# Expert weights of a graph-MoE kernel: adjacent matrix rows per partition, and operands read with a column step

## The reference

```python
logits = x @ Wg + bg
vals, idx = jax.lax.top_k(logits, TOP_K)
gates = jax.nn.softmax(vals, axis=-1)
...
h1 = jax.nn.gelu(jnp.einsum('ecd,edh->ech', h, w1) + b1[:, None, :], approximate=False)
h2 = jnp.einsum('ech,ehd->ecd', h1, w2) + b2[:, None, :]
...
return jnp.zeros((N, D), x.dtype).at[tok_s].add(g_s[:, None] * y_s)
```

## Time and profile before

| | us |
|---|---|
| median of 3 runs | 3404.27 |
| lowest and highest run | 3402.09, 3410.98 |
| the profiled execution's own time | 3410.98 |
| its span, first to last instruction | 3410.9 |
| expert stage in it | 657 (2560 to 3217) |

### The profile page before, as it was taken

The page is one execution under the profiler, slowest core; times in us unless marked ns, Lnnn a source line. Parts: engine busy times, 40 slices in busy tenths (PEclk is TensorE's granted clock), DMA queues, the critical chain, the costliest instruction groups (busy, mean ns, idle before and its releaser), DMA issues.

```text
span 3410.9 us, 46164 instructions
## 1 busy us (share of the span) xinstructions
PE 2063.6 (61%) x10294; PEld 1676.9 (49%) x10295; DVE 1397.3 (41%) x3217; ACT 527.2 (15%) x1404; POOL 2391.6 (70%) x2216
## 2 busy tenths in 40 slices
PE   2222355566655656666566667777767788888550
PEld 2221243444444445455454555555546677777540
DVE  9999211112222333333343444444551122222277
ACT  4443000000000000000010111111112122222113
POOL 6776577777777777777777777777745566666612
PEclk6555677777777888878888888888888899998875
DMA  7000433333333333333333333333323455555432
GB/s 257 0 0 14 130 98 97 98 96 98 99 97 98 100 96 101 101 99 102 98 101 98 102 101 102 98 102 99 101 77 114 129 169 158 165 161 164 148 108 75
DMA packets 205280, 362.36 MB, mean 106 GB/s; under 512 B 43336, under 2 KB 126070, under 8 KB 205054
## 3 DMA queue, kind: packets, MB, share of 16 engines
q0 software_dynamic: 93888, 230.63, 23.6%
q1 hardware_dynamic: 104110, 123.31, 11.4%
q10 hardware_dynamic: 7056, 6.43, 0.5%
HBM read 328.57 MB, written 57.52 MB: 113 GB/s over the span
## 4 chain that ended last, share of the span: by engine, by line
POOL 53%; issue 23%; DVE 9%; PE 7%; DMA 3%; POOLq 2%; DVEq 1%; ACT 1%; PEld 0%; SPq 0%; PEldq 0%; ACTq 0%
POOL ring L473 25%; POOL stage L473 23%; DVE stage L783 4%; POOL ring L500 3%; PE bank L1293 3%; PE bank L1287 2%; DMA ring<-nodes,slot_idx 2%; POOL y L516 2%; DVE acc L1070 1%; DVE stage L786 1%; DMA stage<-y 1%; POOLq L549 1%; DVE stage L806 1%; PE bank L1280 1%; PEld bank L1365 0%
## 5 line engine op out<-in xcount | busy, mean ns | idle before, releaser
L473 POOL DMA_INDIRECT ring<-table,ring_idx x792 | 857.5, 1083 | 274.8 <-issue 240.5
L473 POOL DMA_INDIRECT stage<-table,ring_idx x776 | 820.5, 1057 | 236.4 <-issue 236.4
L1178 PE MATMUL bank<-stage 128*128 128x257 f32 x1040 | 313.4, 467 | 204.2 <-DMA stage<-table,ring_idx 191.9
L1178 PE MATMUL bank<-ring,hot 128*128 128x257 f32 x1056 | 316.2, 464 | 187.9 <-DMA ring<-table,ring_idx 168.1
L1178 PEld LDWEIGHTS bank<-stage 128*128 128x128 f32 x1040 | 243.4, 240 | 269.1 <-issue 185.0
L1178 PEld LDWEIGHTS bank<-ring,hot 128*128 128x128 f32 x1056 | 245.0, 238 | 253.3 <-issue 163.4
L975 DVE TENSOR_TENSOR acc<-acc,bank 128x257 f32 x196 | 83.0, 423 | 686.2 <-PE bank L1178 658.1
L438 POOL TENSOR_TENSOR stage<-iota_f,acc 128x784 bf16<-128x784 f32 x100 | 226.7, 2285 | 80.9 <-PE bank L1158 68.1
L516 POOL DMA_INDIRECT y<-ring,slot_idx x192 | 191.9, 1000 | 116.2 <-issue 88.6
L1178 PE MATMUL bank<-ring,stage 128*128 128x257 f32 x528 | 175.7, 504 | 148.2 <-DMA ring<-table,ring_idx 123.8
L500 POOL DMA_INDIRECT ring<-nodes,slot_idx x192 | 197.7, 1030 | 96.2 <-POOL slot_idx L496 56.0
(11 more groups left out here) (229 smaller groups left out, 2904.3 us busy)
## 6 DMA issues: line engine op xcount, KB each, us to landing
stage<-in_L_gnn_w_dram SPq DMA_DIRECT2D x128, 512.0 KB
ring<-table,ring_idx POOLq DMA_INDIRECT x792
y<-zeros SPq DMA_DIRECT2D x49, 256.0 KB, 2.1
stage<-y SPq DMA_DIRECT2D x14, 896.0 KB, 7.2
stage<-table,ring_idx POOLq DMA_INDIRECT x776
stage<-in_L_gnn_b_dram SPq DMA_DIRECT2D x64, 128.0 KB
table<-stage SPq DMA_DIRECT2D x7, 896.0 KB, 4.2
nodes<-yS ACTq DMA_DIRECT2D x49, 128.0 KB
```

The lines of the kernel that those rows point to most:

```text
L473: pool.indirect_dma_start(out=ring(q)[:, j, 0:D], out_offset=None, in_=table[:, :], in_offset=bass.IndirectOffsetOnAxis(ap=ring_idx[:, q, ...
L1178: last = pe.matmul(bank[:, 0:D + 1], hots[:, j, :], ring(q)[:, j, :], start=j == 0, stop=j == CPG - 1)
```

## The change

w1 and w2 of an expert are loaded so that partition p holds adjacent rows: rows 2p and 2p+1 of w1, rows 4p to 4p+3 of w2. Each is one run of 4 KB. Token features have to be split over the partitions in the same way, so the transpose for place c reads columns c, c+2, c+4, ... of a token row (a step of two f32, 8 bytes). Hidden unit 4p+j is to stand in partition p of block j, so the first layer's stationary operand takes columns j, j+4, j+8, ... of w1 (a step of four f32, 16 bytes), and b1 is transposed with that step too. All products, their number and order stay.

```diff
+        xg_c = xg.rearrange("p b k (r c) -> p b k c r", c=DK)
+        xgx_c = xgx.rearrange("p (r c) -> p c r", c=DK)
+        w1_j = w1s.rearrange("p b k (m j) -> p b k j m", j=HK)
...
-                sp.dma_start(w1s[:, par, :, :], w1[bass.ds(e, 1), :, :].rearrange("o (k p) h -> p (o k) h", p=P)).then_inc(w1_in[par], 16)
+                sp.dma_start(w1s[:, par, :, :], w1[bass.ds(e, 1), :, :].rearrange("o (p k) h -> p (o k) h", p=P)).then_inc(w1_in[par], 16)
...
-                sp.dma_start(w2s[:, par, :, :], w2[bass.ds(e, 1), :, :].rearrange("o (j p) d -> p (o j) d", p=P)).then_inc(w2_in[par], 16)
+                sp.dma_start(w2s[:, par, :, :], w2[bass.ds(e, 1), :, :].rearrange("o (p j) d -> p (o j) d", p=P)).then_inc(w2_in[par], 16)
...
-                last = pe.transpose(banks[3][:, j * EX:(j + 1) * EX], b1r[:, j * P:(j + 1) * P], ident[0:EX, 0:EX])
+                last = pe.transpose(banks[3][:, j * EX:(j + 1) * EX], b1r.rearrange("e (p j) -> e j p", j=HK)[:, j, :], ident[0:EX, 0:EX])
...
                         last = pe.transpose(banks[k // 2][:, (k % 2) * D + c * P:(k % 2) * D + (c + 1) * P],
-                                            xg[:, par, k, c * P:(c + 1) * P], ident[:, :])
+                                            xg_c[:, par, k, c, :], ident[:, :])
...
-                        last = pe.matmul(bank[:, j * P:(j + 1) * P], w1s[:, par, c, j * P:(j + 1) * P], xt[:, c, :],
+                        last = pe.matmul(bank[:, j * P:(j + 1) * P], w1_j[:, par, c, j, :], xt[:, c, :],
...
-                            last = pe.transpose(banks[1][:, D + c * P:D + (c + 1) * P], xgx[:, c * P:(c + 1) * P], ident[:, :])
+                            last = pe.transpose(banks[1][:, D + c * P:D + (c + 1) * P], xgx_c[:, c, :], ident[:, :])
```

## The result

The changed kernel takes 3524.3 us (median of four runs, 3521.77 to 3532.28), against 3403.9 us before: the ratio is 1.0354, with a 95% interval of 1.0339 to 1.0370. It is 120 us slower. The forecast was no change, 3402 us; the time is that of the rival with doubled weight loads, 3521 us.

What follows compares the result with a forecast made beforehand. The prediction took POOL's issue of indirect DMAs to pace the expert stage. Its terms, -2 + 0 + 0, took the profiled 3411 us to 3409; against the 3404.27 median it gave 3402 us, range 3388 to 3540.

Steps and rivals of the forecast that it cites:

- the rival with doubled weight loads: First layer's stepped weight loads take twice as long: 222 us more PE work, +117, about 3521 us; chance 0.26.
- What bounds the stage: Expert stage: paced by POOL's issue of indirect DMAs, sixty-two rounds of 9.6 us, 595 of the 657 us.
- Weight transfers: Loads of w1 and w2: 432 packets per expert after 944, 10 us less engine time; taken as -2 us.
- the line through two other stretches: Packet cost fitted to stretches of mostly 2 KB and 1 KB packets: 0.0316 ns per byte, 151 ns for 4 KB.
- Tokens with a step of two: Token transposes, 384 loads: taken as 0, up to +5 us; at twice the pace 42 us, within PE's slack.
- Layer-1 weights: First layer's 1984 weight loads with a step of four: taken as nothing; upper bound, each load twice as long.
- The rival's sum: Doubled first-layer loads: 222 us of PE work, 85 filling gather waits, 20 back from clock: +117, about 3521 us.
- the stated range: Range around the doubled-loads rival's 3521 us: 3495 to 3555 us; chance 0.26.
- The point from which it decides: PE's room in two-chunk rounds: 1.5 us over 32 loads, some 45 ns per load hidden; beyond it every ns counts.

## Why the prediction was wrong

**What bounds the stage: right.** More work on POOL went into the stage of the kernel before nearly whole (235 of 253 us), less work shortened the kernel by 98 us.

**Weight transfers: right, but for a term's size.** 432 packets per expert came out, and hardly a change in time from them (0.9972 with long runs alone, 0.9997 with those of w1). The saving was 1.7 us of engine time per expert and not 10: with 6.8 us for b2 taken off (128 packets at the 53 ns of the earlier trace rows), a 4 KB packet cost some 53.0/256 = 0.21 us (an estimate) in the stage, beside other traffic, where the line through two other stretches gave 0.151. Nothing hung on it.

**Tokens with a step of two: right.** The pace of the transposes is (0.87 - 0.283)/5 = 0.117 us, against 0.110: nothing that shows.

**Layer-1 weights: the step that failed.** The term was put at nothing because "the load seems to take a value only every second clock, and the reading of SBUF may keep up with a step as it is". The rows behind it, 186 against 137 ns, show how long loads without a step last. They say nothing of how fast columns in separate stretches of 16 bytes can be read. They are no rates either: loads of 192 ns follow each other every 0.111 us, and the transposes, whose loads last 137 ns, are no closer together, at 0.11. The runs put 1.8 ns per stretch in its place: 128 stretches are 0.23 us, so the term is 236 us of PE work. Nor is this price paid in TensorE's clocks. In the first loads of the changed kernel, with PE idle for 10.9 and 1.5 us before, the granted clock is 0.50, and a load lasts as long as at full clock:

```profile
2553.00:2559.00 6.00, 5.89 (x25) 5.89 (x26) 0.00 (x0) 1.14 (x4) 4.08 (x6) 0.50 0.13 33
...
L1291 PEld LDWEIGHTS bank<-ring,stage x26: 308/329/329, 2553.1 to 2558.9; 128*128 128x128 f32 x26
```

(2558.9 - 2553.1)/25 = 0.232 us apart, against 0.230 at full clock, while loads without a step go from 192 to 333 ns and from 0.111 to 0.224 us apart at that clock. So an argument in clocks could not have decided it. What the rows did show, that the load already set the pace of the first layer so that any added time would be on PE's path, was right and spoke for the rival.

The Trainium skill, SBUF — State Buffer (section "Door 1: The DMA port swizzle", its note on cachelines), asks for two accesses in each 16-byte line for full bandwidth. The runs agree for TensorE: a step of two f32 has two and costs 6 ns per load, a step of four has one and doubles it. The same note's words that strides of up to four f32 are free are not borne out, at 0.172 us for three and 0.230 us for four. The prediction had named both readings and gave more weight to the wrong one.

**The rival's sum: right in total, off in its terms.** It had 222 us of added PE work, less 85 of waits for gathers, less 20 of clock: +117. Measured are 236 of work; PE's busy time grew by only 188, so 48 came back, and its idle time gave 70. 188 - 70 is 118, the growth of the stage. That 117 and 118 agree so closely is luck, since three errors cancel. The 48 us can be placed by line: the second layer's matmuls went from 248 to 222 us in all and the transposes from 69 to 57, at the higher clock; the first layer went from 246 to 472, by 226 and not 236, since its loads that had run at half clock hardly got longer. The time lay inside the stated range.

**The point from which it decides: right in kind, rough in size.** The prediction put 45 ns per load under cover. A step of two adds 6 ns and costs nothing. A step of three adds 61 ns, the step of four on half of the loads 60 on average; beyond 45 ns that is 1984 x 0.015 = 30 us, and the stages grew by 32 and 30. But for the whole change the same rule gives 1984 x (0.119 - 0.045) = 147 us, where 118 were measured, so it isn't exact, and the close agreement of the two smaller cases is in part luck.

## What to carry to other kernels

A contiguous transfer isn't worth a stepped matmul operand: look which side is short of time before moving a rearrangement from DMA to TensorE. If an operand must have a step, count the 16-byte stretches that its columns touch; for f32 two columns in each was nearly free here, and one in each took twice as long, for the stationary and the moving operand alike. And where two engines' rounds are close, work out which paces the stage: the same 236 us of work cost 118, 212 or nothing here, by what POOL did beside it.

## What the runs showed of the hardware

- A TensorE operand of f32 is read at 1.8 ns (1.77 to 1.84) per 16-byte stretch of a partition, as soon as this is slower than the pace without a step (0.111 us per load, 0.216 per matmul with 256 moving columns). It was so for weight loads (64, 96 and 128 stretches) and for a moving operand (256), and a step of eight cost what a step of four did. For the step of four it was the same at a granted clock of 0.50 and of 1.00.
- A drain on GpSimd behind indirect gathers ended some 0.4 us after the last of them had landed, in the four rounds looked at. It took 2.6 us on average in one kernel, whose gathers land in 3.5 us, and 1.9 in the other, where they land in 2.7.
- Hardware queue packets of 4 KB took about 0.21 us each in the stage (an estimate from its share and count); transfers of the same bytes in a quarter to half of the packets took nearly the same engine time, 59.8 against 61.5 us per expert.
